# Attention by image groups instead of by whole batch, with the layer normalisation ahead of it cut in four

## The reference, cut to what matters

```python
h = h + attn(layernorm(h))                       # h: 32 images x 141 tokens x 64
qkv = x @ Wqkv + bqkv
q, k, v = jnp.reshape(qkv, (3, b, n, d, h))      # 8 heads of 64
score = jnp.einsum('bnqh,btqh->bnth', q, k) * d ** (-0.5)
attn = jax.nn.softmax(score, axis=1)             # over the first token index n
av = jnp.einsum('bnnh,bnqh->bnqh', attn, v)      # only the diagonal of attn is used
out = av.reshape(b, n, d * h) @ W0 + b0
```

## Time and profile before

| | us |
|---|---|
| median of three runs | 2692.91 |
| the profiled execution | 2692.11 |
| its span | 2690.3 |
| normalisation and turning of tokens, 2049 to 2094 | 45 |
| four head pairs, 2094 to 2349 | 255 |
| output product, 2349 to 2382 | 33 |
| turning back and adding, 2382 to 2388.6 | 6.6 |

### The profile page before, as it was taken

How to read it: one execution, slowest core, us unless ns; L and a number is a source line. 1 busy time by engine, 2 the same in 40 slices (tenths; PEclk the granted TensorE clock), 3 DMA queues, 4 the chain that set the end, 5 groups by cost and what they waited for, 6 DMA issues and landing times. The chain is left out here.

```text
span 2690.3 us, 75014 instructions
## 1 busy us (share of the span) xinstructions
PE 2267.7 (84%) x32251; PEld 1466.2 (54%) x32251; DVE 1704.0 (63%) x2585; ACT 1717.2 (64%) x2771; POOL 191.9 (7%) x237
## 2 busy tenths in 40 slices
PE   7679989966997997699899859996993777765999
PEld 4556657754664776566567656662221666642444
DVE  4767878884776887577778757771005776634443
ACT  2823358875776887667678766777992777721333
POOL 0000000000000000000000000000002222202443
PEclk9889989998998999899999989998996899976999
DMA  5746577558997774799977379996541000012332
GB/s 173 237 144 219 213 275 258 192 191 277 360 347 281 279 248 153 247 350 361 335 266 259 124 249 328 366 341 233 179 140 35 1 1 1 1 26 63 88 87 60
DMA packets 179062, 537.18 MB, mean 200 GB/s; under 512 B 23183, under 2 KB 38223, under 8 KB 178511
## 3 DMA queue, kind: packets, MB, share of 16 engines
q1 hardware_dynamic: 178735, 532.38, 58.6%
HBM read 362.57 MB, written 170.37 MB: 198 GB/s over the span
## 5 line engine op out<-in xcount | busy, mean ns | idle before, releaser
L398 PE MATMUL P<-cst,mem 128*128 128x128 f32 (+1 forms) x3760 | 528.8, 284 | 54.2 <-ACT mem L661 13.9
L643 ACT ACTIVATE mem<-P,small 128x512 f32<-128x512 f32 x512 | 323.7, 684 | 365.0 <-PE P L505 279.6
L398 PEld LDWEIGHTS P<-cst,mem 128*128 128x128 f32 (+1 forms) x3760 | 412.1, 143 | 175.7 <-issue 123.0
L505 PEld LDWEIGHTS P<-cst,mem 64*128 64x128 f32 x4096 | 251.2, 188 | 212.8 <-DVE mem L774 107.1
L786 DVE BATCH_NORM_STATS2 mem<-mem 128x6 f32<-128x512 f32 x512 | 327.1, 681 | 42.4 <-ACT mem L643 41.4
L816 DVE COPY mem<-P 128x512 f32<-128x512 f32 x384 | 247.9, 686 | 100.4 <-PE P L398 99.1
L505 PE MATMUL P<-cst,mem 64*128 64x128 f32 x4096 | 301.1, 286 | 1.2 <-issue 1.1
L779 DVE COPY mem<-P 128x512 f32<-128x512 f32 x256 | 174.9, 686 | 144.7 <-PE P L486 144.7
L633 ACT ACTIVATE mem<-mem,small 128x1024 f32<-128x1024 f32 x192 | 237.9, 1239 | 37.4 <-DMA mem<-z_d 37.4
L774 DVE COPY mem<-P 128x512 f32<-128x512 f32 x256 | 176.7, 690 | 114.0 <-PE P L398 113.9
L661 ACT ACTIVATE mem<-mem,small 128x1024 f32<-128x1024 f32 x192 | 232.6, 1248 | 7.7 <-DMA mem<-z_d 6.7
(11 more groups left out here) (167 smaller groups left out, 3096.8 us busy)
## 6 DMA issues: line engine op xcount, KB each, us to landing
mem<-z_d SPq DMA_DIRECT2D x384, 512.0 KB, 5.3
z_d<-mem SPq DMA_DIRECT2D x256, 512.0 KB, 6.7
mem<-in_wmix SPq DMA_DIRECT2D x64, 1024.0 KB, 8.7
G_d<-mem SPq DMA_DIRECT2D x128, 256.0 KB, 4.0
mem<-G_d SPq DMA_DIRECT2D x128, 256.0 KB, 5.5
hz<-z_d SPq DMA_DIRECT2D x64, 512.0 KB, 4.6
mdB<-dT_d SPq DMA_DIRECT2D x44, 384.0 KB, 5.6
mem<-in_x SPq DMA_DIRECT2D x128, 12.0 KB
```

Source lines behind the costliest of these rows:

```text
L398: return nc.tensor.matmul(out, in_, ident[0:n, 0:n], start=True, stop=True, is_transpose=True)
L505: last = nc.tensor.matmul(banks[x][:, j * 128:j * 128 + 128], ATs[o, a.q % 2, j * 128:j * 128 + 128], i2c[o, x * 128:x * 128 + 128], start ...
L643: nc.scalar.activation(ychunk(a, h), P[4 + 2 * (a.q % 2) + h][:, :], ACT.Identity, bias=bias0 if first else pwb_c).then_inc(S["eY"], 1)
```

## The change

`build_attention` is written anew. What it does now:

- Normalisation in four chunks (three of 12 token rows of a partition, one of 11). VectorE keeps mean, subtraction, sum, reciprocal and multiplication; the square (L1181) and the second copy (L1189) go to ScalarE, and TensorE starts to turn a chunk when it is there. `xT` now holds the same tokens in both halves of the partitions, and VectorE (L1254) and ScalarE (L1193) copy every other tile of it.
- 16 steps g: four groups of eight images times four head pairs. Per step nine projection products of 376 columns, plain float32 on 64 rows (L1109), on alternating halves of the partitions and in two PSUM banks (0 and 1) in turn. VectorE alone moves them out (L1271), to `Q`, `K` and `V`, which are kept in two sets.
- Scores (L1099) have the keys on the partitions: one matmul of 128 keys x 141 queries per image and head, in three rounds of 3, 3 and 2 images; the last 13 keys of four images go together as 32-row pieces in a fourth round. The two heads lie on the two halves of the partitions and write to two banks.
- VectorE takes the maxima (L1278) and ScalarE the exponentials and sums (L1202), written back into PSUM, since nothing reads them afterwards.
- The own scores come another way: GpSimd multiplies q by k (L1064), TensorE sums each head's 64 rows with a two-column matrix (L1118, L1122), and one small chain per step, for all 20 columns at once, subtracts the maximum, clips at zero, takes the exponential and multiplies by the reciprocal (L1285 to L1295).
- Spreading (L1137, L1140): a weight column repeated 64 times is the stationary operand, an identity the moving one. VectorE multiplies into v (L1301).
- The output product (L1151) is done per group of images, in the pipeline, two steps after the group's last head pair, from bank 6, which spreading also uses.

The steps are pipelined in the written order: in iteration g and each of its four rounds TensorE does the scores of step g-1, projections of step g, own scores of step g-1 and a spreading tile of step g-2.

```diff
+        NG, GB, GT, COLS = 16, 8, 8 * SEQ, 20
+        CHUNKS_J = [(k, min(k + 12, PER)) for k in range(0, PER, 12)]
+        UNITS = [(0, 1, 2), (3, 4), (5, 6), (7, 8)]
+        ROUNDS = [(0, 1, 2), (3, 4, 5), (6, 7), (0, 1)]
+        TILES = [(0, 3), (3, 6), (6, 8)]
...
-            nc.gpsimd.memset(KZ[:, :, :, :], 0.0).then_inc(S["zero"], 1)
+            for g in range(NG):
+                pool.wait_ge(S["ev"], 9 * g + 6)
+                if g >= 2:
+                    pool.wait_ge(S["sd"], g - 1)
+                nc.gpsimd.tensor_tensor(QK[:, g % 2, 0:GT], Q[:, g % 2, 0:GT], K[:, g % 2, 0:GT], ALU.mult).then_inc(S["qk"], 1)
...
+            def scores(g, rho):
+                if rho == 0:
+                    pe.wait_ge(S["ev"], 9 * g + 6)
+                n = 4 * g + rho
+                if n >= 2:
+                    pe.wait_ge(S["exp"], 2 * n - 2)
+                banks = P[2 + rho % 2 * 2:4 + rho % 2 * 2]
...
+                            if rho == 3:
+                                out, keys = banks[h][32 * j:32 * j + 32, o], K[r, g % 2, t + 128:t + 160]
+                            else:
+                                out, keys = banks[h][:, o], K[r, g % 2, t:t + 128]
+                            last = nc.tensor.matmul(out, keys, Q[r, g % 2, t:t + SEQ], start=True, stop=True)
+                last.then_inc(S["sc"], 1)
...
+            def project(g, rho):
+                r, hp = g // HP, g % HP
+                for u in UNITS[rho]:
+                    n = 9 * g + u
+                    if n >= 2:
+                        pe.wait_ge(S["ev"], n - 1)
+                    half, t = slice(n % 2 * 64, n % 2 * 64 + 64), u // 3 * THIRD + r * NT
+                    nc.tensor.matmul(P[n % 2][:, 0:NT], wq[half, u % 3 * HP + hp, :], xT[half, t:t + NT], start=True, stop=True).then_inc(S["qkv"], 1)
...
+            def own_scores(g, rho):
+                if rho == 0:
+                    pe.wait_ge(S["qk"], g + 1)
...
+                for b in (2 * rho, 2 * rho + 1):
+                    last = nc.tensor.matmul(P[7][:, o + 2 * b:o + 2 * b + 2], QK[:, g % 2, b * SEQ:b * SEQ + 128], heads, start=True, stop=True)
...
+            def spread(g, i):
+                n = 3 * g + i
+                if i == 0:
+                    pe.wait_ge(S["aw"], g + 1)
+                if n:
+                    pe.wait_ge(S["av"], n)
+                if i == 0 and g:
+                    pe.wait_ge(S["oA"], outputs_before(g))
...
+                        nc.tensor.matmul(P[6][w, o:o + 128], aw[:, g % 2, 2 * b + h:2 * b + h + 1].broadcast_to([128, D]), ident, start=True, stop=True)
...
+            for g in range(NG + 4):
+                for rho in range(4):
+                    if 0 <= g - 1 < NG:
+                        scores(g - 1, rho)
+                    if g < NG:
+                        project(g, rho)
+                    if 0 <= g - 1 < NG:
+                        own_scores(g - 1, rho)
+                    if rho == 0 and output_at(g) is not None:
+                        outputs(*output_at(g))
+                    if rho and 0 <= g - 2 < NG:
+                        spread(g - 2, rho - 1)
...
+            def sums_of(g, rho):
+                for h in range(2):
+                    act.wait_ge(S["max"], 8 * g + 2 * rho + h + 1)
...
+                        last = nc.scalar.activation(bank[:, k * SEQ:k * SEQ + SEQ], bank[:, k * SEQ:k * SEQ + SEQ], ACT.Exp, bias=nmax[:, g % 2, c:c + 1], accum_out=sums[:, g % 2, c:c + 1])
+                    last.then_inc(S["exp"], 1)
...
+            for g in range(NG + 4):
+                for rho in range(4):
+                    if rho == 0 and 0 <= g - 2 < NG:
+                        dve.wait_ge(S["sd"], g - 1)
...
+                        dve.wait_ge(S["exp"], 8 * (g - 1))
+                        link(nc.vector.reciprocal(sums[:, g % 2, :], sums[:, g % 2, :]))
+                    if 0 <= g - 1 < NG:
+                        maxima(g - 1, rho)
+                    if g < NG:
+                        evict(g, rho)
+                    if rho == 0 and 0 <= g - 2 < NG:
+                        dve.wait_ge(S["ea"], g - 1)
+                        nc.vector.tensor_tensor(aw[:, g % 2, :], ea[:, g % 2, :], sums[:, g % 2, :], ALU.mult).then_inc(S["aw"], 1)
+                    if rho and 0 <= g - 2 < NG:
+                        m, (lo, hi) = g - 2, TILES[rho - 1]
+                        dve.wait_ge(S["sp"], 3 * m + rho)
...
+                        nc.vector.tensor_tensor(v, P[6][:, 0:(hi - lo) * SEQ], v, ALU.mult).then_inc(S["av"], 1)
```

More of the change, by code:

```diff
@@ L846, in attention_constants @@
 def attention_constants():
[L848 to L853, removed]
+    p = np.arange(128)
+    heads = (p[:, None] // 64 == np.arange(2)[None]) * 1.0
+    fill = np.zeros((128, PER + 128 - 2))
+    order = np.tile(np.arange(EXPERTS, dtype=np.float64), (128, 1))
+    return np.concatenate([heads, fill, order, np.eye(128)], axis=1).astype(np.float32)
 NACONST = PER + 128 + EXPERTS + 128
@@ L1058, in tiled, with output_at, outputs_before @@
-        def tiled(tile, x):
-            return tile if x == 0 else tile.rearrange("p (b i) -> p b i", i=PER)
+        CHUNKS_J = [(k, min(k + 12, PER)) for k in range(0, PER, 12)]
+        UNITS = [(0, 1, 2), (3, 4), (5, 6), (7, 8)]
+        ROUNDS = [(0, 1, 2), (3, 4, 5), (6, 7), (0, 1)]
+        TILES = [(0, 3), (3, 6), (6, 8)]
+        def output_at(g):
+            r, i = (g - 6) // HP, (g - 6) % HP
+            return (r, i) if 0 <= r < PAIRS // HP and i < 2 else None
+        def outputs_before(g):
+            return sum(output_at(t) is not None for t in range(g + 3))
@@ new lines, in project @@
+            def project(g, rho):
[9 more added lines that the diff above has]
+                    pe.wait_ge(S["qk"], g + 1)
+                    if g:
+                        pe.wait_ge(S["t1"], g)
+                o = g % 2 * COLS
+                for b in (2 * rho, 2 * rho + 1):
+                    last = nc.tensor.matmul(P[7][:, o + 2 * b:o + 2 * b + 2], QK[:, g % 2, b * SEQ:b * SEQ + 128], heads, start=True, stop=True)
+                if rho == 3:
+                    for b in range(GB):
+                        j, c, t = 32 * (b % 4), o + 16 + b // 4 * 2, b * SEQ + 128
+                        last = nc.tensor.matmul(P[7][j:j + 32, c:c + 2], QK[:, g % 2, t:t + 32], heads, start=True, stop=True)
+                    last.then_inc(S["sd"], 1)
@@ L1130, in _, with outputs @@
+            def outputs(r, i):
+                pe.wait_ge(S["av"], min(3 * (4 * r + 4 + i), 3 * NG))
+                if i:
+                    pe.wait_ge(S["oA"], 2 * r + 1)
+                tiles = TILES[0:2] if i == 0 else TILES[2:3]
                 for hp in range(HP):
-                    last = nc.tensor.matmul(P[i % 2][0:D, 0:(hi - lo) * PER], w0s[:, hp, :], VT[:, hp, lo * PER:hi * PER], start=hp == 0, stop=hp == HP - 1)
+                    for w, (lo, hi) in enumerate(tiles):
+                        last = nc.tensor.matmul(P[6][w * 64:w * 64 + 64, 0:(hi - lo) * SEQ], w0s[:, hp, :], V[:, r % 2, hp, lo * SEQ:hi * SEQ], start=hp == 0, stop=hp == HP - 1)
```

304 lines of the change are left out of this document (136 added, 168 removed).

## The result

The changed kernel takes 2661.53 us, the median of four runs (2647.15 to 2662.93); the kernel before, on the same chip, 2690.82 (2685.74 to 2693.61). The ratio is 0.9883, interval 0.986 to 0.9907. The forecast was 2627: the direction is right and the time lies in the range, but the gain is 29 us where 65 were forecast. The profile is of the execution of 2662.93, the slowest of the four.

The account below looks back on a forecast made before the run. VectorE alone held the normalisation, engines took turns setting the pace in the loop, and TensorE worked almost alone in the output. Savings of 22 + 43 = 65 us: 2692.1 - 65 = 2627 us, range 2598 to 2672.

Parts of the forecast that it names:

- Normalisation: Normalisation and turning of tokens ahead of the first projection: 23 us instead of 45, 22 us saved.
- A step: One pipelined loop step, summed over four rounds: 13.4 us, bounds 12.0 (TensorE never waits) and 15.5 (VectorE's handovers exposed).
- The own scores: TensorE's two-column matmuls in a step: 16 records at 0.055 us, with 16 short tails 1.2 us.
- the shape changes: TensorE changing the shape of its pieces 13 times a step, 0.15 us each: 2.0 us.
- GpSimd's product: GpSimd's one product of 1128 columns per step: at most 4.7 us, with two rounds for it.
- rival 2: VectorE bounds the loop: 15.5 us a step, 2660 us; chance 0.26 with what lies between it and 2680.
- Rival 4: TensorE's pieces take turns or its clock stays at 1.2 GHz: about 21 us a step, 2745; 0.08 shared with another rival.
- round 0: First round of a step: 4.0 us, TensorE standing for some 1.5 of it, the stall that replaces the old one.
- its forecast of 245.2: Loop with output products: 6.5 + 13 + 187.6 + 14.7 + 16 + 7.4 = 245.2 us against 288, 43 us saved.
- from the first projection to the second L1285: Loop start: first projections alone 6.5 us at the low clock, second iteration 13, then one step of 13.4.
- the stretch of 13 steps: Second to fifteenth L1285 of the loop, with three output products: 13 x 13.4 + 14.7 = 188.9 us.
- the end: After the last projections: two iterations of scores, own scores and spreading 16 us, last output product with evictions 7.4.

Follow-up runs that it names:

- e5: Changed kernel with the normalisation in whole passes again, ScalarE doing only the square root; single xT and loop kept: 2644.94 us, ratio 0.985.
- e12: e7 with ScalarE doing four of the nine projection evictions (units 0, 3, 5 and 7): 2616.04 us, ratio 0.9735.
- e1: Changed kernel plus one unused full-array matmul of 376 columns per step, just before the wait for the third projection's bank: 2637.28 us, ratio 0.9819.
- e7: Changed kernel with a round's own scores and output product issued ahead of its third projection, no work added: 2625.97 us, ratio 0.9764.
- e9: Changed kernel plus the extra matmul of e1, but in round 2 ahead of spreading, the stall kept: 2663.35 us, ratio 0.9918.
- e15: The kernel of e7 measured again: 2621.05 us, ratio 0.9757.
- e8: e7 with ScalarE evicting the first projection (unit 0) of each step: 2623.89 us, ratio 0.9768.
- e14: The kernel of e12 measured again: 2627.49 us, ratio 0.9769.
- e11: e7 with two more VectorE reductions of 423 values in round 0, so the third projection waits again: 2652.8 us, ratio 0.9875.
- e6: Changed kernel with the nine projections dealt to the rounds as 2, 2, 2, 3 instead of 3, 2, 2, 2: 2641.94 us, ratio 0.9851.
- e3: Changed kernel with seven of the eight full-size own-score matmuls of a step left out, results wrong: 2617.3 us, ratio 0.9747.
- e13: As e1, but three matmuls of two moving columns fill the stall instead of one of 376 columns: 2642.52 us, ratio 0.983.

## Why the prediction was half right

**Normalisation: right.** The first projection starts 23.1 us after the stage begins (23 forecast), 22.0 saved. The reasoning was right in sum and partly wrong in its parts: the prediction counted the square at 4.4 and the copy at 5.0 as work that goes. In e5, with GpSimd at rest, they are 3.29 and 1.75; 4.4 us of the old stage would have gone without touching either. The last section shows what GpSimd did beside them.

**A step: right, by terms that made up for each other.** 13.3 at full clock, forecast 13.4, with TensorE 12.1 (12.0). The own scores were mis-sized: 0.135 us for each record of two columns (four records 0.54 apart), where L1348's 0.083 at the low clock was taken for 0.055; 2.4 us a step instead of 1.2. The trace has a weight load of 128 columns for each (L1118 PEld), with idle time of issue ahead of it, which suggests that the two moving columns are the least of it. In return less is left for the shape changes, as far as a difference can tell: 12.1 - 10.0 - 1.2 = 0.9 where 2.0 were put down. Evictions (0.603), maxima (0.594), v (0.599) and exponentials in PSUM (0.352) are as forecast. GpSimd's product takes 2.58 us, under the bound of 4.7.

**VectorE as the bound (rival 2): wrong.** e12 took four of its nine evictions away, and a step went from 12.8 to 12.5, no further than with one. The total came out at 2660 as this rival has it, but for another reason; without the profile the right number would have confirmed the wrong cause.

**The clock: the step that failed.** Rival 4 had it, "the granted clock stays at its lower level", and it was set aside with: "The next loop has shorter idle times." The sentence doesn't follow from the prediction's own round 0, in which TensorE stands for 1.5 us at a time, against the 1.00 of the earlier trace rows. The sum then took full clock from the second iteration on. By parts, of the 42.8 us that the loop took over its forecast of 245.2:
- from the first projection to the second L1285: 45.6 instead of 6.5 + 13 + 13.4 = 32.9, 12.7 more, the clock low until 2108;
- the stretch of 13 steps: 209.5 instead of 188.9, 20.6 more, the falls;
- the end: 32.9 instead of 16 + 7.4 = 23.4, 9.5 more, the clock low for 24 us.

Not all of it hangs on the stall. With the stall filled and the clock at 1.00 in the stretch (e1) the loop is 256.7: 31.3 of the 42.8 come back. The start is still 3.7 over its forecast (36.6) and the end 8.1 (31.5, with a granted clock of 0.67). These two terms of the sum were too small by themselves: from the second iteration on they were counted at full clock, and the clock is low in the end of every kernel here, e7's too.

The argument compared idle shares (1 us in 4.15 before, 1.16 in 13.3 now) and concluded that less idle time is safer. It isn't so here: a fall follows the 1.16 us stall in a TensorE that is 91 percent busy. Shown by five kernels: filled (e1) the clock holds; the same work elsewhere (e9) and it falls; shortened to 0.62 or less by order (e7, e15, and e8, e12, e14) and it holds; put back (e11) and it falls; moved to another round (e6) and the falls move too. With the clock held the time is 2637 with a superfluous matmul, 10 over the forecast of 2627. That e7 and e15 come out at 2621 to 2626 is luck as far as the forecast goes: their order shortens the stretch to 178.0, 10.9 under its forecast, and that makes up for the start and the end. The Trainium skill (TensorE: Matmul & The Clock Gate, A second HAM failure mode: psum-queue depth-cycling) describes a kernel in which TensorE "micro-idles between MM groups frequently enough that HAM oscillates" (HAM is what sets TensorE's clock); the trace agrees, with 0.89 over the 13 steps and one idle time of 1.16 us in each. The prediction did not weigh it.

The loop before did not keep its clock either. The forecast looked at 2111 to 2151, where it is 1.00. At the end of each of the four head pairs, where TensorE waits 1.94 us instead of 1.00, it fell for 7 to 10 us (from 2154.6, 2216.2, 2281.0 and 2345.8), 31 us in all. The first of them:

```profile
2154.03 1.16 PE L1125 MATMUL AP<-aD,ac 96*128 96x423 f32 x2 [1.94 <-DVE aD L1226]
```

```profile
2147.10:2154.60 7.50, 4.55 (x29) 3.45 (x27) 4.65 (x10) 5.41 (x30) 3.14 (x6) 1.00 0.00 1
2154.60:2161.60 7.00, 5.66 (x17) 4.81 (x16) 4.00 (x8) 2.85 (x6) 0.00 (x0) 0.51 0.01 4
```

What stays open: why an idle time of 1.00 in each 4.15 us left the clock alone there and 0.70 in each 13.6 us of e6 does not; whether the thin matmuls right behind the stall count as less work (e3 says they aren't needed, e13 hints that they fill poorly); and what decides at which of the 13 steps it falls, since most passed the same stall without a fall.

The version that beats both kernels is e7: 0.9764 and 0.9757 in two measurements.

## What to carry to other kernels

A short, regular stall on TensorE costs more than its length if the clock falls behind it: here 1.16 us in each 13.3 cost 20.6, 16.4 and 3.0 us in 13 steps of three executions. Look at the granted clock of every step, and put work that doesn't depend on the slow engine between the producer and the wait, before asking for a faster eviction. Compare several executions, since one profile can show many falls or few. When a forecast rests on a clock staying up, give the fall its own chance and price, even where TensorE looks nearly full, and read the clock of the whole old loop, not of its best stretch.

## What the runs showed of the hardware

- The granted clock fell from 2.4 to 1.2 GHz with TensorE 91 percent busy, one idle time of 1.16 us ahead of it, and stayed down for 17 us in which TensorE was busy all the time (2190 to 2207). In e6 an idle time of 0.70 was enough.
- A float32 matmul with 128 stationary and two moving columns takes 0.135 us for each of its two records at full clock; seven such matmuls are 1.7 us of a step (e3).
- GpSimd seems to have held VectorE up in the stage before. What it did there, by start and length, and the two passes of VectorE that were longer than in e5:

```profile
2053.47 3.62 POOL L1075 CAST awh<-aQ 128x1536 fp32r<-128x1536 f32 x1 [222.03 <-DMA ab<-in_b]
2057.18 6.34 POOL L1077 TENSOR_TENSOR awl<-aQ,awh 128x1536 fp32r<-128x1536 f32 x1
2063.47 7.77 POOL L1078 MEMSET aKZ<- 128x9216 f32 x1
```

```profile
2055.81 4.43 DVE L992 TENSOR_TENSOR aV<-aV 96x3008 f32<-96x3008 f32 x1
...
2067.82 5.03 DVE L997 COPY aV<-aV 96x3008 f32<-96x3008 f32 x1
```

The square ends 3.15 us after the cast beside which it began (2057.09), the copy 1.61 after the clearing (2071.24). That is about what each takes alone in e5, 3.29 and 1.75: they look as if they had stood still until GpSimd's instruction was over. The multiplication of L996, which lay beside the same clearing, took 3.29 and wasn't held. The Trainium skill (SBUF — State Buffer, SBUF: two separate sides) says that certain VectorE operations and GpSimd take a shared pair of ports for a whole instruction and the other one blocks; the trace agrees, at 3.28 us for the copy and 1.14 for the square. No run changed this alone.
- ScalarE's exponential of 141 columns takes 0.352 us from PSUM to PSUM (128 partitions), no more than the 0.380 from PSUM to SBUF before (96 partitions).
